# Four fc1 blocks in a row and one quantization for all of them, in the MLP stage of a transformer layer

## The reference

```
x = x + attn(layernorm(x))     # 16 heads of 64; keys and values come from 128 summaries,
                               # each the mean of 64 layer-normed tokens (127 of them; the first is one token)
x = x + ffn(layernorm(x))

def block_quant(v):            # per block of 32 elements along K
    amax  = max(|v|) over the block
    e     = floor(log2(max(amax, 2**-126)))
    scale = exp2(e - 3)
    return round(v / scale) * scale

h = block_quant(x) @ block_quant(w_fc).T + b_fc      # 1024 -> 4096
h = gelu(h)
y = block_quant(h) @ block_quant(w_proj).T + b_proj  # 4096 -> 1024
```

## Time and profile before

| quantity | value |
|---|---|
| time, median of 3 runs | 2857.09 us (2856.69 to 2858.22) |
| time of the profiled execution | 2858.71 us |
| its span, slowest core (core 5) | 2857.1 us; all cores 2844.2 to 2857.1 us |
| PE, DVE, ACT busy | 1034.3 us (36%), 1071.6 us (38%), 518.6 us (18%) |
| chain that ended last | PE 33%, DVE 31%, ACT 13%, issue 13%, DMA 8% |
| PE matmuls of the projection (L994) | 1024, 302.2 us |
| DMA | 106.58 MB, mean 37 GB/s |

### The profile page before, as it was taken

How to read it: one execution, slowest core, us unless ns; L and a number is a source line. 1 busy time by engine, 2 the same in 40 slices (tenths; PEclk the granted TensorE clock), 3 DMA queues, 4 the chain that set the end, 5 groups by cost and what they waited for, 6 DMA issues and landing times.

```text
span 2857.1 us, 17726 instructions; the slowest of 8 cores (2844.2 to 2857.1 us)
## 1 busy us (share of the span) xinstructions
PE 1034.3 (36%) x5088; PEld 468.3 (16%) x5088; DVE 1071.6 (38%) x2181; ACT 518.6 (18%) x934; POOL 40.1 (1%) x60
## 2 busy tenths in 40 slices
PE   1111111111123333422334255554445444555545
PEld 0000000100011211111112022221222212222212
DVE  4555555665600311213112433333433343333333
ACT  1111111111101312113021122212222122222122
POOL 0000000000000000000000000000000000000000
PEclk9999999999996566655665577776777667777767
DMA  3222222222232022130220100000000000000000
GB/s 74 59 59 54 61 63 72 70 71 74 59 59 61 13 74 44 26 78 15 74 45 15 45 15 15 15 15 0 15 15 15 15 15 15 15 15 15 15 0 15
DMA packets 38399, 106.58 MB, mean 37 GB/s; under 512 B 5520, under 2 KB 5536, under 8 KB 36256
## 3 DMA queue, kind: packets, MB, share of 16 engines
q0 software_dynamic: 19392, 37.77, 8.2%
q1 hardware_dynamic: 18912, 67.68, 6.8%
HBM read 126.42 MB, written 16.78 MB: 50 GB/s over the span
## 4 chain that ended last, share of the span: by engine, by line
PE 33%; DVE 31%; ACT 13%; issue 13%; DMA 8%; DVEq 1%; SPq 0%; ACTq 0%; POOLq 0%
PE psC L994 11%; PE psE L242 4%; DVE wstr L400 3%; DVE qa_amax L322 3%; DVE qa_amax L972 3%; DMA wbuf<-wq_in 2%; PE psB L938 2%; PE psA L938 2%; ACT hqT L250 2%; PE psA L942 2%; PE psB L942 2%; DVE bnscr L473 2%; DVE hqb L224 1%; DVE hbuf L221 1%; DVEq L1037 1%
## 5 line engine op out<-in xcount | busy, mean ns | idle before, releaser
L994 PE MATMUL psC<-wpjTq,hqT 128*128 128x512 bf16 x1024 | 302.2, 459 | 64.1 <-ACT hqT L250 64.1
L972 DVE TENSOR_REDUCE qa_amax<-hbuf 128x32 f32<-128x1024 f32 x64 | 75.0, 1214 | 330.6 <-ACT hbuf L958 298.4
L242 PE MATMUL psE<-ident,wqnat 128*128 128x128 bf16 x256 | 37.4, 300 | 356.0 <-DVE qa_e L350 330.6
L242 PE MATMUL psE<-ident,hqb 128*128 128x128 bf16 x256 | 31.1, 260 | 358.9 <-DVE hqb L224 358.9
L994 PEld LDWEIGHTS psC<-wpjTq,hqT 128*128 128x128 bf16 x1024 | 111.4, 114 | 233.1 <-issue 169.9
L766 DVE TENSOR_TENSOR ebuf<-ebuf,mask_sb 128x2048 bf16<-128x2048 bf16 x16 | 19.6, 1226 | 344.8 <-ACT ebuf L757 318.8
L517 PE MATMUL psA<-xsq,patt 128*128 128x512 bf16 x64 | 37.5, 585 | 291.6 <-DVE meanb L514 291.6
L250 ACT ACTIVATE hqT<-psE 128x512 bf16<-128x512 f32 x64 | 38.2, 597 | 382.3 <-PE psE L242 382.3
L938 PE MATMUL psA<-wfcTq,xqfm 128*128 128x512 bf16 x256 | 98.1, 383 | 0.9 <-ACT xqfm L250 0.9
L942 PE MATMUL psA<-wfcTq,xqfm 128*128 128x512 bf16 x256 | 97.8, 382 | 0.0
L938 PE MATMUL psB<-wfcTq,xqfm 128*128 128x512 bf16 x256 | 97.4, 380 | 0.0
(11 more groups left out here) (235 smaller groups left out, 1994.5 us busy)
## 6 DMA issues: line engine op xcount, KB each, us to landing
xsq<-xseq POOLq DMA_DIRECT2D x32, 512.0 KB, 6.4
wstr<-wfc_in SPq DMA_DIRECT2D x32, 512.0 KB, 4.3
wstr<-wpj_in SPq DMA_DIRECT2D x16, 1024.0 KB, 6.0
xring<-xown SPq DMA_DIRECT2D x16, 512.0 KB, 5.6
wbuf<-wq_in POOLq DMA_DIRECT2D x8, 1024.0 KB, 8.4
wbuf<-wo_in POOLq DMA_DIRECT2D x8, 1024.0 KB, 8.4
xmid_scr<-xmid_t SPq DMA_DIRECT2D x16, 512.0 KB, 2.7
x2r<-xmid_scr SPq DMA_DIRECT2D x16, 512.0 KB, 4.0
```

The costliest lines, as they stand in the source:

```text
L242: E.matmul(d, s, ident[:, :], start=True, stop=True),
L972: S.op("vector", lambda E, v=hg, o=32 * gi: E.tensor_reduce(out=qa_amax[:, o:o + 32], in_=v, axis=AXX, op=ALU.max, apply_absolute_value=Tr ...
L994: S.op("tensor", lambda E, c_=c, cc=cl, cjj=cj, s_=gs: E.matmul(psC[:, cc:cc + 512], hqT[:, 1024 * s_ + 128 * cjj:1024 * s_ + 128 * cjj + ...
```

## The change

There are three parts.

1. The floor under the block maximum (a DVE operation on `qa_amax`, L178 and L326) goes; instead a per-partition constant `TINYpp` of 2**-100 is added inside the logarithm, as its bias operand.
2. The two multiplications that make `qa_eb` from the scale (L210 and L213; L379 and L382) become one DVE instruction with two operations.
3. Stage 3 is rewritten. `hbuf` holds four blocks. `p2_pair` goes; `p2_back` issues the fc1 blocks 1 to 3 one behind the other, with a GELU behind each, `p2_front(t + 1)` between fc1 of block 3 and its GELU, then one reduction and one `quant_consts` over all 128 blocks of 32 elements, then four times quantize, transpose and project. The `outb` buffer goes: the residual sum is written in place into `x2r` and stored from there, so the load of a tile now waits for the store of the tile two before it (`ST0`/`ST1`).

```diff
         def quant_consts(nb, amax_ap, e_ap, s0_ap, s_ap, m_ap, eb_ap):
-            S.op("vector", lambda E, a=amax_ap: E.tensor_scalar(
-                out=a, in0=a, scalar1=float(2.0**-100), scalar2=None, op0=ALU.max), inc="VE")
             w("scalar", "VE")
             S.op("scalar", lambda E, a=amax_ap, e=e_ap: E.activation(
-                out=e, in_=a, func=ACT.Ln), inc="AE")
+                out=e, in_=a, func=ACT.Ln, bias=TINYpp[:, :], scale=1.0), inc="AE")
...
             S.op("vector", lambda E, s=s_ap, eb=eb_ap: E.tensor_scalar(
-                out=eb, in0=s, scalar1=K2, scalar2=None, op0=ALU.mult), inc="VE")
-            S.wait_at("vector", "VE", S.c("VE"))
-            S.op("vector", lambda E, eb=eb_ap: E.tensor_scalar(
-                out=eb, in0=eb, scalar1=Dt[:, :], scalar2=None, op0=ALU.mult), inc="VE")
+                out=eb, in0=s, scalar1=K2, scalar2=Dt[:, :], op0=ALU.mult,
+                op1=ALU.mult), inc="VE")
...
         def p2_front(t):
             buf = x2r0 if t % 2 == 0 else x2r1
-            S.wait_at("sync", "VE", S.c("VE"))
+            st_sem = "ST0" if t % 2 == 0 else "ST1"
+            S.wait_at("sync", st_sem, S.c(st_sem))
...
+        def p2_back(t, do_front):
+            p2_gelu(t, 0)
+            if (t, -1) in ae_gmark:
+                S.wait_at("tensor", "AE", ae_gmark[(t, -1)])
+            p2_fc1(t, 1)
+            p2_gelu(t, 1)
+            S.wait_at("tensor", "AE", ae_gmark[(t, 0)])
+            p2_fc1(t, 2)
+            p2_gelu(t, 2)
+            S.wait_at("tensor", "AE", ae_gmark[(t, 1)])
+            p2_fc1(t, 3)
             if do_front:
                 p2_front(t + 1)
-            w("vector", "AE")
-            for gi, g in enumerate((g0, g1)):
+            p2_gelu(t, 3)
+            ae_g3 = ae_gmark[(t, 3)]
+            S.wait_at("vector", "AE", ae_g3)
+            hh = hbuf.ap().rearrange("p (b e) -> p b e", e=32)
+            S.op("vector", lambda E, v=hh: E.tensor_reduce(
+                out=qa_amax[:, 0:128], in_=v, axis=AXX, op=ALU.max,
+                apply_absolute_value=True), inc="VE")
+            ve_red = S.c("VE")
+            S.wait_at("vector", "VE", ve_red)
+            quant_consts(128, qa_amax[:, 0:128], qa_e[:, 0:128], qa_s0[:, 0:128],
+                         qa_s[:, 0:128], qa_m[:, 0:128], qa_eb[:, 0:128])
+            for g in range(4):
...
                 S.wait_at("vector", "PE", S.c("PE"))
                 quant_apply(hg, hg, qg, ebg)
...
             w("vector", "PE")
-            oslot = t % 2
             buf = x2r0 if t % 2 == 0 else x2r1
-            S.wait_at("vector", "ST0" if t % 2 == 0 else "ST1",
-                      S.c("ST0" if t % 2 == 0 else "ST1"))
-            S.op("vector", lambda E, b=buf, o=oslot: E.tensor_tensor(
-                out=outb[:, o * D:(o + 1) * D], in0=psC[:, :], in1=b[:, :], op=ALU.add), inc="VE")
+            S.op("vector", lambda E, b=buf: E.tensor_tensor(
+                out=b[:, :], in0=psC[:, :], in1=b[:, :], op=ALU.add), inc="VE")
```

More of the change, by code:

```diff
@@ L110, in build_nc @@
         EB1pp = sb("EB1pp", [128, 1], F32)
+        TINYpp = sb("TINYpp", [128, 1], F32)
         bnscr = sb("bnscr", [128, 12], F32)
@@ L130, in build_nc @@
         wbuf = sb("wbuf", [128, 4 * D], BF16)
[L132 to L137, removed]
+        qa_amax = sb("qa_amax", [128, 160], F32)
+        qa_e = sb("qa_e", [128, 160], F32)
+        qa_s0 = sb("qa_s0", [128, 160], F32)
+        qa_s = sb("qa_s", [128, 160], F32)
+        qa_m = sb("qa_m", [128, 160], F32)
+        qa_eb = sb("qa_eb", [128, 160], F32)
         a2c = sb("a2c", [128, 1], F32)
@@ L324, in stage_R @@
                 apply_absolute_value=True), inc="VE")
[L325 to L328, removed]
         def stage_L(i):
@@ L334, in stage_L @@
             S.op("scalar", lambda E, o_=o, nb_=nb: E.activation(
-                out=qa_e[:, o_:o_ + nb_], in_=qa_amax[:, o_:o_ + nb_], func=ACT.Ln), inc="AE")
+                out=qa_e[:, o_:o_ + nb_], in_=qa_amax[:, o_:o_ + nb_], func=ACT.Ln,
+                bias=TINYpp[:, :], scale=1.0), inc="AE")
         def stage_E1(i):
@@ L380, in stage_S @@
                     out=qa_eb[:, o_:o_ + nb_], in0=qa_s[:, o_:o_ + nb_], scalar1=K2,
[L381 to L384, removed]
+                    scalar2=Dt[:, :], op0=ALU.mult, op1=ALU.mult),
                 lambda E, o_=o, nb_=nb: E.tensor_tensor(
@@ L914, in p2_front @@
             S.wait_at("vector", "VE", S.c("VE"))
-            o = 96
+            o = 128
             v3 = xln2.ap().rearrange("p (b e) -> p b e", e=32)
@@ L951, in p2_fc1 @@
                 start=False, stop=True), inc="PE")
+        ae_gmark = {}
         def p2_gelu(t, g):
             dst = psA if g % 2 == 0 else psB
-            gs = g % 2
             w("scalar", "PE")
             S.wait_at("scalar", "VE", S.c("VE"))
-            S.op("scalar", lambda E, d=dst, s_=gs: E.activation(
+            S.op("scalar", lambda E, d=dst, s_=g: E.activation(
                 out=hbuf[:, s_ * D:(s_ + 1) * D], in_=d[:, :], func=ACT.Gelu), inc="AE")
[L961 to L965, removed]
+            ae_gmark[(t, g)] = S.c("AE")
@@ L969, in p2_pair @@
-            for gi, g in enumerate((g0, g1)):
-                gs = g % 2
[L971 to L975, removed]
-            quant_consts(64, qa_amax[:, 0:64], qa_e[:, 0:64], qa_s0[:, 0:64],
-                         qa_s[:, 0:64], qa_m[:, 0:64], qa_eb[:, 0:64])
@@ L978, in p2_pair @@
-            for gi, g in enumerate((g0, g1)):
-                gs = g % 2
-                hg = hbuf.ap()[:, gs * D:(gs + 1) * D].rearrange("p (b e) -> p b e", e=32)
-                ebg = qa_eb.ap()[:, 32 * gi:32 * gi + 32].unsqueeze(2).broadcast_to([128, 32, 32])
+            p2_gelu(t, 3)
[5 more added lines that the diff above has]
+                apply_absolute_value=True), inc="VE")
@@ L985, in p2_pair @@
                 S.wait_at("tensor", "VE", S.c("VE"))
+                if g == 0 and (t - 1) in ve_rmark:
+                    S.wait_at("tensor", "VE", ve_rmark[t - 1])
                 transpose8(lambda j: hqb[:, 128 * j:128 * j + 128],
```

23 lines of the change are left out of this document (12 added, 11 removed).

## The result

| quantity | before | after |
|---|---|---|
| time, median of 8 runs each | 2858.05 us (2856.69 to 2860.78) | 2610.25 us (2608.10 to 2611.84) |
| ratio, 95% interval | | 0.9132, 0.9122 to 0.9142 |
| span, slowest core | 2857.1 us (core 5) | 2609.6 us (core 2); all cores 2598.7 to 2609.6 us |
| PE, DVE, ACT busy | 1034.3, 1071.6, 518.6 us | 965.7, 1005.5, 516.7 us |
| chain that ended last | PE 33%, DVE 31%, ACT 13%, issue 13%, DMA 8% | PE 32%, DVE 27%, issue 16%, ACT 14%, DMA 9% |

The forecast was 2618 us with 2598 to 2650 as its range, so it held, 8 us too slow. The views that answer to those of before follow. First the page's head and the residual sum of stage 3, as in the earlier trace rows: duration in ns min/median/max, first and last start.

A forecast was written before the change was run, and what follows sets the result against it. PE, ACT and DVE take turns, so a tile is a sum of steps, going from 78.5 to 65.2 us. Stage 3's 212 plus the prologue's 27 save 239 from 2857.1: 2618 us forecast, range 2598 to 2650 for 8 in 10.

The forecast's parts named there:

- 8, second and third: Stage 3, projections of blocks 1 and 2 at the upper clock level: 5.17 us each, ending at 59.2.
- 9, fourth: Stage 3, projection of block 3 with its two bias matmuls: 6.00 us, ending the tile at 65.2.
- Steps 1 to 6: Stage 3 tile, from fc1 of block 0 to the first transposes of the quantized GELU output: 41.4 us.
- Step 5: Stage 3, end of reduction to first quantizing subtraction: 5.5 us, including 0.5 for widening from 64 to 128 blocks.
- Step 3: Stage 3, fourth GELU waits on ACT behind the front part and ends last; DVE's reduction can start at 28.6 us.
- Step 7: Stage 3, first projection, from its transposes to the next block's: 7.5 us, taken from 7.11 and 7.91 before.
- Stage 3: Total saving claimed for stage 3: 212 us; 14 periods give 186, last tile 11.8, tile 0 13.5 plus 0.5.
- The load behind the store: Stage 3, the tile load's wait for the store is covered by 3 us before ACT is free: costed at nothing.
- Prologue: Prologue, dropped DVE operations shorten each of 48 jobs by 0.52 to 0.62 us: 25 to 30, taken as 27.
- the third rival: Prologue operations were covered, with weight loads or transposes ending last in most jobs: 27 us stay, 2645 us; chance 9%.
- The clock rivals: Stage 3's long dense PE stretch loses its clock: a quarter paid, near 2690 us, 5%; all paid, 2905 us, 2%.
- the peak-current limiter: Rule against the forecast: dense matmuls on a third core bring 13/16 clock; 4 us a tile, about 2684 us.

The follow-up runs named there:

- the run with 38 extra matmuls: 38 matmuls with unused results added behind the next tile's transposes, against the version with front part two tiles ahead and a reduction per block: 2375.46 us.

## Why the prediction was right, step by step

The steps, in us from the start of fc1 of block 0, and what the trace of the changed kernel has (steps 1 to 3 from the first half of the tile at 2421.48, 4 to 9 from the second half of the one before it):

| step | forecast | measured |
|---|---|---|
| 1, third GELU starts | 12.53 | 12.50 |
| 2, front part ends | 26.2 | 26.18 |
| 3, reduction starts | 28.6 | 28.61 |
| 4, reduction of 128x4096 | 4.4 | 4.42 |
| 5, exponents | 5.5 | 5.52 |
| 6, quantize to transposes | 2.82 | 2.91 |
| 7, first projection | 7.5 | 6.80 (6.76 to 6.99 in 15 tiles, 7.35 in the last) |
| 8, second and third | 5.17 each | 5.16, 5.17 |
| 9, fourth | 6.00 | 5.99 |
| tile | 65.2 | 64.85 (mean of fourteen) |
| last tile | 54.4 | 54.25 |

- **Steps 1 to 6** came out within 0.1 us each. They were sums of rows of the same instructions in the same order of waits. Step 5 also held a choice that no row gave, 0.5 for the wider blocks out of 0 to 0.6 (2 at the most); that it came out so close has some luck in it. In half of the tiles the first transposes come 0.2 to 0.4 later than here, in four of them since the reduction already starts late, so that they stand at 41.6 in the mean, against 41.4. Step 3 carries the theory, since it says that the fourth GELU ends last because it stands behind the front part; putting it ahead moved the transposes by 1.5 us, as worked out.
- **Step 7** was mis-sized: 0.5 to 0.7 us too long. I took the mean of two gaps of the old kernel, 7.11 and 7.91, as if it were a property of the projection. It goes by how long the clock stays at the lower level after the transposes (back at 1.00 after 5.1 us with a gap of 6.9, after 7.3 with one of 8.0), and that differs from version to version and from tile to tile (gaps of 6.7 to 8.3 in these runs without extra matmuls). In the old kernel's second half the clock was back at 2701.2, not at about 2700.5 as the prediction reads it; its sum doesn't use that. Why the clock comes back when it does stays open. With 6.9 in the mean it took 0.6 off the tile, of which the late first transposes gave 0.2 back: the 5 us by which the 14 periods came out below the forecast. The same term explains the misses of 6 to 13 us in five of the experiments.
- **Stage 3** saved 218.5: fourteen periods of 13.7 (191.7), the last tile 11.9, and tile 0 with its front part 14.9 (95.1 from its first statistics to its residual before, 80.2 after). Forecast 212.
- **The load behind the store** was covered, as costed. The statistics start 7.4 us into the tile (forecast 8.9; 9.5 in the one behind the longest store) and end at 9.3 (forecast: at most 11.7), 5.6 ahead of ACT, and taking the wait away changed nothing.
- **Prologue**: forecast 27, range 25 to 30. The trace has 27.5 at the last of the summaries and 29.1 at the first statistics of stage 3, and 0.61 for the one job compared above, times 48 is 29. Of the 0.31 for the floor I gave 0.21 to 0.31 and took near the middle; it was 0.30. DVE's waits for a weight load came to 6.4 us in 5 places, against 4.6 in one before: the third rival had 2 us in it.
- **The clock rivals** (2690 and 2905) had nothing for them. In the earlier trace rows the upper level could be seen for 20 us; now it holds for the 30 us of the last three rows shown, and the changed kernel's trace has only the two levels on all eight cores. By the peak-current limiter of the Trainium skill ("TensorE: Matmul & The Clock Gate", Part 1) the time would have been about 2684, an estimate; it was 2610. The level of 13/16 does exist here: in the run with 38 extra matmuls the clock was granted at 0.81 once on each of cores 4 to 7, for 2.7 to 3.7 us, and on core 6 the 16 matmuls of a projection took 3.90 us in it instead of 3.61. No other trace has it.

Where the time came from, shown by the two runs with one part each: 54 us from the small DVE operations (30 of them before stage 3), 192 from the rewritten stage 3.

## What to carry to other kernels

In a kernel where the engines take turns, write one period as a sum of steps from rows of the same instructions: eight of nine steps were right to 0.1 us in the tile shown. Where a step begins behind an idle PE, give it the duration at both clock levels, since a shorter chain ahead of it may be followed by a slower projection. And look for the longest step that is in the period only because of its place: moving the next tile's front part beside the last projection (with the fourth GELU ahead of it), and three reductions beside fc1, was worth 208 us more, somewhat above the 192 of the rewritten stage 3.
